# An attention layer with a written-out job order: row maxima stored in query order, and one PSUM bank moved from the scores to the other jobs

## The reference

```
xn = layernorm(x)                                  # (1, 2048, 256)
k, q, v = (einsum('ihd,bpd->biph', W, xn) for W in (W_K, W_Q, W_V))
scores = einsum('biph,biqh->biqp', k, q)           # causal mask, -1e10 above the diagonal
attn = softmax(masked(scores) / sqrt(128), axis=-1)
z = einsum('biqp,biph->biqh', attn, v)
s = einsum('df,bqf->bqd', W_O, z_flat)
g = silu(xn @ W_base.T + b_base + 2 * (expert e = argmax(xn @ router_W.T): Bw[e] @ (A[e] @ xn)))
out = x + s * g
```

## Time and profile before

| | us |
|---|---|
| median of 3 runs | 1548.5 |
| lowest and highest | 1548.2, 1549.68 |
| the profiled execution, its own time | 1548.1 |
| its span in the trace | 1546.2 |
| PE busy | 1459.5 (94%) |
| ACT busy | 1274.0 (82%) |
| DVE busy | 1248.1 (81%) |
| POOL busy | 793.4 (51%) |

### The profile page before, as it was taken

How to read it: one execution, slowest core, us unless ns; L and a number is a source line. 1 busy time by engine, 2 the same in 40 slices (tenths; PEclk the granted TensorE clock), 3 DMA queues, 4 the chain that set the end, 5 groups by cost and what they waited for, 6 DMA issues and landing times.

```text
span 1546.2 us, 23204 instructions
## 1 busy us (share of the span) xinstructions
PE 1459.5 (94%) x7788; PEld 1193.2 (77%) x7788; DVE 1248.1 (81%) x2541; ACT 1274.0 (82%) x2196; POOL 793.4 (51%) x688
## 2 busy tenths in 40 slices
PE   5999999999999999999999999999999999999997
PEld 4877778777877878777787777877787777877765
DVE  6788877888788886888868887788878898788864
ACT  2788898889888898898988888888987988888962
POOL 2444655455465555456554555554645555544740
PEclk9899999999999999999999999999999999999998
DMA  2100010000100001000010001000010000100002
GB/s 75 49 8 14 15 25 25 15 15 8 29 21 15 15 7 42 15 14 13 10 42 15 7 15 28 22 15 14 8 35 21 15 7 13 40 8 15 15 28 82
DMA packets 30070, 33.75 MB, mean 22 GB/s; under 512 B 11008, under 2 KB 17664, under 8 KB 29952
## 3 DMA queue, kind: packets, MB, share of 16 engines
q1 hardware_dynamic: 29952, 32.26, 8.3%
HBM read 30.02 MB, written 2.23 MB: 21 GB/s over the span
## 4 chain that ended last, share of the span: by engine, by line
PE 51%; ACT 24%; DVE 13%; issue 9%; POOL 2%; DMA 0%; SPq 0%; ACTq 0%; POOLq 0%; DVEq 0%
PE ps L281 15%; PE ps L282 14%; PE ps L283 14%; ACT ps L478 7%; ACT probs L498 7%; ACT p_hi L499 6%; DVE p_lo L551 6%; PE ps L719 4%; DVE partmax L566 3%; POOL colsum L433 2%; PE ps L754 2%; ACT qT_hi L486 1%; DVE z_lo L588 1%; ACT z_hi L504 1%; PE ps L731 1%
## 5 line engine op out<-in xcount | busy, mean ns | idle before, releaser
L433 POOL TENSOR_TENSOR colsum<-colsum,probs 128x512 f32<-128x512 f32 (+3 forms) x512 | 610.2, 1192 | 388.3 <-ACT probs L498 373.6
L478 ACT ACTIVATE ps<-maxrow 128x512 f32<-128x512 f32 (+3 forms) x640 | 645.3, 1008 | 8.9 <-DMA maxrow<-max_dram 8.7
L551 DVE TENSOR_TENSOR p_lo<-probs,p_hi 128x512 fp32r<-128x512 f32 (+3 forms) x640 | 614.9, 968 | 42.4 <-ACT p_hi L499 41.4
L498 ACT ACTIVATE probs<-ps 128x512 f32<-128x512 f32 (+3 forms) x640 | 362.9, 567 | 141.4 <-PE ps L731 74.8
L499 ACT ACTIVATE p_hi<-ps 128x512 fp32r<-128x512 f32 (+3 forms) x640 | 365.3, 571 | 0.0
L566 DVE TENSOR_REDUCE partmax<-ps 128x1 f32<-128x512 f32 x384 | 256.9, 679 | 10.4 <-PE ps L719 9.5
L281 PE MATMUL ps<-qT_hi,kT_hi 128*128 128x512 f32 (+3 forms) x640 | 247.6, 387 | 12.7 <-ACT ps L478 9.6
L281 PE MATMUL ps<-p_hi,v_hi 128*128 128x512 f32 (+3 forms) x640 | 241.7, 378 | 13.2 <-DVE p_lo L551 12.2
L282 PE MATMUL ps<-qT_lo,kT_hi 128*128 128x512 f32 (+3 forms) x640 | 234.3, 366 | 0.0
L283 PE MATMUL ps<-qT_hi,kT_lo 128*128 128x512 f32 (+3 forms) x640 | 233.9, 366 | 0.0
L282 PE MATMUL ps<-p_lo,v_hi 128*128 128x512 f32 (+3 forms) x640 | 233.5, 365 | 0.0
(11 more groups left out here) (106 smaller groups left out, 2174.8 us busy)
## 6 DMA issues: line engine op xcount, KB each, us to landing
maxrow<-max_dram SPq DMA_DIRECT2D x64, 256.0 KB, 3.8
wraw<-wqk_dram SPq DMA_DIRECT2D x16, 256.0 KB, 3.8
acc<-x_dram SPq DMA_DIRECT2D x4, 512.0 KB, 7.2
wraw<-wv_dram SPq DMA_DIRECT2D x8, 256.0 KB, 4.7
wraw<-wo_dram SPq DMA_DIRECT2D x8, 256.0 KB, 2.9
probs<-x_dram SPq DMA_DIRECT2D x4, 512.0 KB, 4.5
out_dram<-acc SPq DMA_DIRECT2D x4, 512.0 KB, 3.0
max_dram<-rowmax SPq DMA_DIRECT2D x64, 2.0 KB, 1.4
```

Of the source, the lines that this page charges most:

```text
L433: nc.gpsimd.tensor_tensor(total[:, c0:], total[:, c0:], tile[:, c0:], ALU.add)\
L478: nc.scalar.activation(st[job.n % SCORE_BANKS].rearrange("p (t n) -> p t n", t=TB)[:, q:, :], maxrow[:, job.g, :].rearrange("p (n t) -> p ...
L498: nc.scalar.activation(probs[:, k, c0:], src, ACT.Exp, scale=SCALE).then_inc(probs_ready, 1)
L551: nc.vector.tensor_tensor(p_lo[:, k, c0:], probs[:, k, c0:], f32(p_hi[:, k, c0:]), ALU.subtract)\
```

## The change

Four edits.

1. L341 writes `rowmax` to `max_dram` so that the row lies in query order. Before, it lay as (p t), each partition's four values side by side; now it lies as (t p), and each of the 512 values goes to an address of its own.
2. The seed (L478) reads `maxrow` with step one; before it read with a step of four elements.
3. `SCORE_BANKS` goes from 3 to 2 and `AUX_BANKS` from 3 to 4. The seed of tile n waits for `hi_ready` of n - `SCORE_BANKS` + 1, that is, now for the `p_hi` that stands directly ahead of it on ACT. The banks of `Base` are now the two score banks and both `zb` banks, so `Base` also waits for the last `z_lo`.
4. The string `SCHEDULE` is another order of the same jobs.

```diff
-SCORE_BANKS = 3
+SCORE_BANKS = 2
-AUX_BANKS = 3
+AUX_BANKS = 4
...
 SCHEDULE = (
-    "V00 w Pq03 V01 w w z7 | | Pk02 | s7 Pk03 v V11 | o70 v M0222 | M0212 o71 v M0202 M0232 v | V21 S0 Z0 | v V10 "
...
-    "Z1 M0322 v | M0312 | M0332 M0310 v | O10 Pk10 M0320 v M0331 v M0333 | | v V31 | Pk11 V20 v v M1030 | | M1100 "
-    "v M1120 v | | O11 v M1111 S2 v | M1010 | v v M1000 | M1020 M1130 Pq12 | Z2 v v | V30 M1230 v | M1110 | O20 v "
-    "| v v M1200 | M1210 v | Pk12 | v M1101 | M1131 M1121 v M1231 | v | M1202 v | v M1201 | Pq13 O21 v | M1211 "
...
+    "Pq03 V00 w V10 w | V01 w M0311 | z7 Pk02 | v s7 | o70 v M0330 M0232 o71 | M0300 M0212 v v M0202 | M0222 S0 "
...
+    "M1020 v v | O11 | v | v | M1000 v v | M1030 Z2 Pq12 | v | V31 v V30 M1131 M1121 | v v | | M1111 v M1211 S2 "
+    "M1210 v M1120 | O20 v | O21 | v | v M1130 M1230 Pk12 | v M1231 v | M1201 M1101 M1222 | v | M1232 v | v v | v "
...
-                    sp.dma_start(row.rearrange("(p t) -> p t", t=TB), rowmax[:, job.g, :]).then_inc(max_out, 16)
+                    sp.dma_start(row.rearrange("(t p) -> p t", p=P), rowmax[:, job.g, :],
+                                 allow_slow_non_contiguous=True).then_inc(max_out, 16)
...
-                q = columns(job) // P
-                nc.scalar.activation(st[job.n % SCORE_BANKS].rearrange("p (t n) -> p t n", t=TB)[:, q:, :],
-                                     maxrow[:, job.g, :].rearrange("p (n t) -> p t n", t=TB)[:, q:, :],
-                                     ACT.Copy, scale=-1.0).then_inc(seeded, 1)
+                c0 = columns(job)
+                nc.scalar.activation(st[job.n % SCORE_BANKS][:, c0:], maxrow[:, job.g, c0:], ACT.Copy, scale=-1.0)\
+                  .then_inc(seeded, 1)
...
                 elif isinstance(job, Base):
                     pe.wait_ge(ffn_w_ready, DC + 2)
                     pe.wait_ge(hi_ready, PAIRS * TILES)
+                    pe.wait_ge(z_lo_ready, PAIRS * GROUPS)
                     base(job.b, range(TB))
```

## The result

The changed kernel takes 1698.9 us in the median of four runs, against 1548.4 for the kernel before; the ratio is 1.097, with a 95% interval of 1.093 to 1.101. The forecast was 1482, in a range of 1448 to 1526, with a chance of 0.06 for slower.

What follows compares the result with a forecast made beforehand. The prediction saw PE leading but held up by about 160 us of waits, with ACT and DVE nearly as busy. Terms -48 + 19 - 30 - 14 + 5 + 1.5 took the 1546.2 us span to 1480; with 1.9 around it, 1482, range 1448 to 1526.

Steps and rivals of the forecast that it cites:

- the landing of the write: Write of the maxima on SP: lands in 2.2 us instead of 1.4, adding 5 us to the time.
- the write is late: Rival, chance 0.05: the maxima write lands in 5.6 us, by number of pieces, delaying maxrow; 1568 us.
- the tight block 1 of the odd heads: Tightest block of the new order: about 4.7 us available where write and read want 6.0; 1.3 late, 8 times.
- The seed: Step-one seeds on ACT take exp's lengths, 44% shorter in total; 48 us off the 108 us on the chain.
- 14 for `p_lo`: Weight loader's 40 waits for p_lo lose 0.35 us each because exps come earlier: 14 us off.
- the delays were coupled: Rival, chance 0.14: unblamed waits dissolve with ACT's relief, 60% of the room goes; 1452 us.
- 160 us of room: PE's waits over the whole kernel: span of 1546.2 us against near 1386 without waits, about 160 us.
- 114 us of named waits: Weight loader's waits with a releaser shown: 46.5 us for seeds, 42.1 for ring banks, 25.1 for p_lo.
- the 1386: Estimated end in us for a PE that never waited: matmul steps, masks and last part, start and end.
- The fourth ring bank: Lets PE run one job further ahead of DVE, cutting waits for ring banks: 30 us off.
- The wait on its own engine: Seed on ACT waits for the p_hi just ahead: 0.18 us per seed, 19 us added.
- The wait of `Base`: At the kernel's end, Base waits for the last z_lo: 1.5 us added.

Runs made afterwards that it cites:

- e6: e3 with 512 pieces of 4 bytes, 64 bytes apart, also written to unread memory beside the old write; 1448.9 us.
- e15: e3 with 128 dense pieces of 4 bytes also written to unread memory beside the old write; 1649.6 us.
- e4: The changed kernel with the old write of 16-byte pieces, seeds kept at step one (so other queries' maxima); 1455.3 us.
- e3: The kernel before with only the step-one seed, write untouched, so queries get other queries' maxima; 1451.9 us.
- e13: e3 with banks 2 + 4 and the wait of Base, on the old order; 1459.7 us.
- e1: The changed kernel with the old write and the old stepped seed; new order, banks 2 + 4 and wait of Base stay; 1554.7 us.
- e12: e3 with 512 dense 4-byte pieces also written behind the read of maxrow, waited for only at the kernel's end; 1489.0 us.

## Why the prediction was wrong

**The step that failed** is the landing of the write: "The new write lies between these; I take 2.2". The bracket was false. The store of the output has as many pieces, but each of 1 KB, so that no two begin within 1 KB. I compared by number, and by e6 and e15 the number is not what costs most. Even the rival for the late write took pieces in proportion to their number, 5.6 us, for its worst. The chip gave 8.4.

**The mechanism of the rival "the write is late" was right.** It named five kinds of block, 40 blocks in all, and ACT waits 40 times; the tight block 1 of the odd heads waits 7.2 to 7.6 us on ACT each of the eight times. It put the price at the lateness of each kind of block. With 8.4 in place of 5.6, its own sum is 8 × (8.4 + 3.8 - 4.7) + 8 × (12.2 - 7) + 24 × (12.2 - 8) = 60 + 42 + 101 = 203 us. On the 1455 us of e4 that makes 1658. The read of 4.8 instead of 3.8 adds a microsecond in 40 waits: 1698, and 1698.9 was measured. This agreement is closer than the sum deserves: half of each lateness was to be covered by queued work, and on the other side PE ran slow after the long gaps. By the traces, the 244 us are 175 us by which PE was idle for longer (207.7 us against 32.8 in e4), nearly all of it in waits for a seed, and 1487.5 - 1419.1 = 68 us by which PE was longer busy with the same matmuls than in e4 (1419.1 us busy at a clock of 0.984, against 0.929). That second part, the clock after a gap, stood nowhere in my working.

**The seed** was right in length (602 ns for a forecast of 600 to 660), and its worth was mis-sized: 48 us, with 14 for `p_lo` and 30 for the ring, against 96 for the step alone. The chain of waits gave ACT's seed 7% and I took 44% of that. But a share of the chain prices the instructions that lie on it, not the delays that they hand on: with shorter seeds DVE got its input earlier, freed the ring earlier, and PE's waits for both went with the one edit. This is the rival "the delays were coupled", priced at 1452 us with a chance of 0.14. Its direction was right, and what spoke for it, 160 us of room against 114 us of named waits, was in the text. That e3 measured 1451.9 is luck: the rival had taken off all the self-waits, which e3 does not have, and the kernel that it describes is e4, at 1455.3. Nor did all of the room go: the span of e3, 1447.1, still lies 61 us above the 1386 that the prediction gave to a PE that never waited, though PE is 98% busy there. Whether these 61 us are waits, or the 1386 was too low, no run shows.

**The fourth ring bank** (30 us) is worth nothing once ACT is relieved (e13). While ACT is not, the waits for the ring at L281 do go, by 30 us (e1, with the new order), but the time does not fall (1.005 instead of a little under 1). I added gains that remove the same waits.

**The wait on its own engine** was right in place and size, 0.15 us of delay against 0.18 forecast. Its price of 19 us was too low where ACT is late: in e1 the waits for seeds grew by 56 us. The new order stands in e1 too and was not tried alone, so how much of this is due to the self-wait is open. The wait of `Base` was right: 1.5 us. The Trainium skill, "ScalarE: Activation LUTs", section "What ACT_TABLE_LOAD costs", has 186 ns + 0.833 ns per column, from which 612 ns for 512 columns is an estimate; the trace agrees at step one (602) and nearly at step two (655), not at step four (1155).

## What to carry to other kernels

Before a transfer is cut into smaller pieces on a path with 5 us to spare, measure its landing alone: here dense 4-byte writes to memory took six times as long as 16-byte ones, and held up the transfers behind them. When an engine of a written-out pipeline is late everywhere, its share of the chain can undercount it, as it did here (48 us against 96); compare the named waits with the whole room above the leading engine's own steps. A stepped read may be mended half way: a step of two elements cost 9% more than step one, a step of four 92%.

## What the chip did that I had not expected

- Small writes to memory slow down with density more than with number: for 512 pieces of 4 bytes at 64, 16, 8 and 4 bytes apart, 2.5, 3.2, 4.4 and 8.2 us from the write to the read behind it (the first three with a second write in it), and 7.5 for 128 dense ones.
- In the block shown, the DMA engines were done with such a write in 1.4 us, and the signal of its landing came 7.0 us later.
- Such a write, waited for by nobody, cost 33 to 37 us through the transfers issued after it (e12).
- PE ran at 1.2 GHz for some microseconds in all 24 places where it had stood idle for 5.3 us or more behind a seed, and at full clock in 10 of 12 where it had stood for 1.5 to 2.9.
- ACT's float32 read of SBUF nearly keeps its pace at a step of two elements (655 ns against 602 for 512 columns) and halves it at four (1155).
